# Turning later inputs and router logits on VectorE and DMA instead of TensorE, in a fused attention and feed-forward layer

## The reference

```python
def _L0_attn_ref(x, gamma, w_qkv, w_out):          # 16 heads of 64, DIM 256
    xn = rms_norm(x, gamma)
    qkv = xn @ w_qkv                                # split into q, k, v per head
    sim = jnp.einsum('bhid,bhjd->bhij', q * scale, k)
    out = jnp.einsum('bhij,bhjd->bhid', jax.nn.softmax(sim, axis=-1), v)
    return out.reshape(b, n, DIM_INNER) @ w_out     # after bringing heads back

def _L0_ffn_ref(x, router_w, w1, b1, w2, b2):       # 8 experts, top 2
    router_probs = jax.nn.softmax(xt @ router_w, axis=-1)
    top_k_probs, top_k_indices = jax.lax.top_k(router_probs, TOP_K)
    top_k_probs = top_k_probs / jnp.sum(top_k_probs, axis=-1, keepdims=True)
    expert_out = jax.nn.gelu(xt @ w1 + b1) @ w2 + b2
    return expert_out * jnp.sum(combine, axis=-1, keepdims=True)   # combine: the two weights

x = x + _L0_attn_ref(_layernorm(x), ...)            # x is (8, 512, 256), float32
x = x + _L0_ffn_ref(_layernorm(x), ...)
```

## Time and profile before

| what | us |
|---|---|
| median of 3 runs (1198.33 to 1198.84) | 1198.48 |
| the profiled execution | 1198.14 |
| its span, first to last instruction | 1196.3 |
| TensorE busy / VectorE / ScalarE / GpSimd | 1183.7 / 961.9 / 884.3 / 640.1 |

### The profile page before, as it was taken

The page is one execution under the profiler, slowest core; times in us unless marked ns, Lnnn a source line. Parts: engine busy times, 40 slices in busy tenths (PEclk is TensorE's granted clock), DMA queues, the critical chain, the costliest instruction groups (busy, mean ns, idle before and its releaser), DMA issues. The chain is left out here.

```text
span 1196.3 us, 29198 instructions
## 1 busy us (share of the span) xinstructions
PE 1183.7 (99%) x11347; PEld 1040.4 (87%) x11347; DVE 961.9 (80%) x1714; ACT 884.3 (74%) x1914; POOL 640.1 (54%) x809
## 2 busy tenths in 40 slices
PE   8999999999999999999999999999999999999999
PEld 6778888888888888888888888888888888988988
DVE  7788789878988888888888888889888987666644
ACT  6888788888887888788888887888888884334432
POOL 5776556555655565556555655555555674222221
PEclk9999999999999999999999999999999999999999
DMA  4222111311121113111311131113111232121100
GB/s 132 66 77 66 34 40 30 95 25 35 36 88 35 37 37 89 37 37 37 89 37 36 37 89 37 36 37 89 37 37 37 72 86 79 36 69 39 36 19 36
DMA packets 35240, 62.91 MB, mean 53 GB/s; under 512 B 5920, under 2 KB 12576, under 8 KB 35104
## 3 DMA queue, kind: packets, MB, share of 16 engines
q1 hardware_dynamic: 35104, 61.05, 19.0%
HBM read 19.08 MB, written 8.39 MB: 23 GB/s over the span
## 5 line engine op out<-in xcount | busy, mean ns | idle before, releaser
L927 POOL TENSOR_SCALAR prob<-prob,rowinv 128x512 f32<-128x512 f32 x512 | 350.2, 699 | 290.6 <-DVE rowinv L1116 290.2
L836 ACT ACTIVATE prob<-ps,negmax 128x512 f32<-128x512 f32 x512 | 347.0, 686 | 34.1 <-DVE negmax L1111 29.7
L1035 DVE TENSOR_TENSOR pT_lo<-ps,pT_hi 128x512 fp32r<-128x512 f32 (+1 forms) x384 | 320.4, 862 | 26.0 <-ACT pT_hi L829 21.3
L1111 DVE TENSOR_REDUCE negmax<-ps 128x2 f32<-128x1024 f32 x256 | 311.1, 1215 | 1.3 <-PE ps L524 1.2
L826 ACT ACTIVATE pT_hi<-ps 128x1024 fp32r<-128x1024 f32 x128 | 131.7, 1029 | 99.3 <-issue 98.7
L552 PEld LDWEIGHTS ps<-identity,prob 64*128 64x128 f32 x4096 | 154.7, 138 | 57.9 <-issue 18.2
L552 PE MATMUL ps<-identity,prob 64*128 64x64 f32 x4096 | 177.1, 226 | 3.4 <-DVE vbuf L1035 2.6
L518 PE MATMUL ps<-nat 64*128 64x512 f32 x1024 | 172.1, 413 | 1.5 <-ACT prob L836 0.5
L566 PE MATMUL ps<-pT_hi,vbuf 128*128 128x256 f32 x1024 | 164.8, 283 | 1.7 <-DVE pT_lo L1035 1.6
L566 PE MATMUL ps<-pT_lo,vbuf 128*128 128x256 f32 x1024 | 164.5, 283 | 0.0
L829 ACT ACTIVATE pT_hi<-ps 128x512 fp32r<-128x512 f32 x256 | 140.4, 610 | 16.5 <-PE ps L552 16.5
(11 more groups left out here) (119 smaller groups left out, 2307.1 us busy)
## 6 DMA issues: line engine op xcount, KB each, us to landing
att_hi_v<-halves_out SPq DMA_DIRECT2D x128, 128.0 KB, 2.3
att_lo_v<-halves_out SPq DMA_DIRECT2D x128, 128.0 KB, 2.3
xres<-in_x SPq DMA_DIRECT2D x8, 512.0 KB, 3.4
x_scratch<-xres SPq DMA_DIRECT2D x8, 512.0 KB, 3.1
out_y<-f_o SPq DMA_DIRECT2D x15, 256.0 KB, 2.0
xin<-in_x SPq DMA_DIRECT2D x7, 512.0 KB, 3.8
wstage<-in_w SPq DMA_DIRECT2D x4, 512.0 KB, 3.6
wstage<-in_w_qkv SPq DMA_DIRECT2D x6, 256.0 KB, 3.1
```

What stands on the lines that cost most here:

```text
L836: act.activation(prob[:, n % NPROB, j * SEQ:(j + 1) * SEQ], ps[:, PS_SCORE[n % 2] + j, :], ACT.Exp, bias=negmax[:, n % 4, j:j + 1], accum_ ...
L927: return pool.tensor_scalar(dst, src, scalar, 1.0, ALU.mult, ALU.mult)
L1035: return dve.tensor_tensor(dst, full, hi, ALU.subtract)
L1111: dve.tensor_reduce(negmax[:, n % 4, :], ps[:, PS_SCORE[n % 2]:PS_SCORE[n % 2] + 2, :], AX.X, ALU.max, negate=True).then_inc(s_max, 1)
```

## The change

The input of the first batch is still transposed by TensorE. For the seven later batches and all chunks, VectorE turns the 32x32 blocks of `xn` in place of it (`turn_input`, two instructions), from SBUF to SBUF into `xblocks`; 16 DMAs on SyncE's queue (`spread_input`) then put the blocks where they belong, into the memory of `xn` itself (`xn_turned`). In attention GpSimd makes the hi part from it (`input_hi`) and VectorE the lo part (`input_lo`) at the end of step 13, and the query block of the next batch waits for that. The statistics and normalisation of the next batch start 4 slots earlier. In the feed-forward part `x2_hi` and `ffn_split` read the turned input in SBUF, behind the fourth gelu and the fourth hidden part of the chunk before. The router's product is turned by VectorE from PSUM (`turn_logits`) and spread by 4 DMAs (`spread_logits`), and the product itself stands right behind the last up block, in chunk 0 where it stood. `halves_out` has one buffer of two parts, and the output blocks of even halves stand two steps apart like the odd ones.

Semaphore declarations, changed constants (`NEXT_LN_SLOT = 9`, `SPLIT_STEP = 13`, `QUAD = 32`) and changed indices are left out.

```diff
@@ -81,10 +83,9 @@
...
     for step in range(FIRST_STEP, LAST_STEP + 1):
-        b, rel = divmod(step, SPB_STEPS)
         blocks = []
         if step == -4:
-            blocks += [(2, "xt", 0, 0), (3, "xt", 0, 1)]
+            blocks += [(2, "xt", 0), (3, "xt", 1)]
         if step == -3:
...
@@ -96,13 +97,10 @@
...
             blocks.append((place, "v", step // 4, 1))
-        if rel == 13 and 0 <= b < B:
-            blocks += [(2, "xt", b + 1, 0), (3, "xt", b + 1, 1)]
         for half in range(2 * B - 1):
             since = step - (8 * half + 11)
-            places = {0: 2, 2: 2, 4: 2, 6: 2} if half % 2 else {0: 2, 3: 3, 4: 2, 6: 2}
-            if since in places:
-                blocks.append((places[since], "out", half, list(places).index(since)))
+            if since in (0, 2, 4, 6):
+                blocks.append((2, "out", half, since // 2))
         for place, *task in sorted(blocks):
@@ -159,6 +157,7 @@
...
         xn = sb("xn", [P, TT, D], F32)
+        xblocks = sb("xblocks", [P, KT, TT, P], F32)
...
-        halves_out = sb("halves_out", [P, 2, 2, SEQ], F32, att)
+        halves_out = sb("halves_out", [P, 2, 2, 2 * P], F32, att)
         att_hi_v = sb("att_hi_v", [P, SEQ], F32, att)
@@ -274,6 +275,15 @@
...
+        def block_rows(g, c):
+            return xblocks[g * QUAD:(g + 1) * QUAD, :, :, c * QUAD:(c + 1) * QUAD].rearrange("p k t q -> p (k t) q")
+        def turned_rows(c, g):
+            columns_of_g = xn_turned[c * QUAD:(c + 1) * QUAD].rearrange("p k (t q) -> p (k t) q", t=TT)
+            return columns_of_g[:, :, g * QUAD:(g + 1) * QUAD]
+        N_SPREAD = 16 * (P // QUAD) ** 2
         def aux_bank(block_no):
@@ -366,8 +376,15 @@
         def ln_task(slot):
...
-            b, step = divmod(slot - LN_SLOT, SPB)
-            return (b + 1, step) if step < 9 and 0 <= b + 1 <= B else None
+            if slot < FIRST_SLOT + SPB // 2:
+                return (0, slot - FIRST_SLOT) if 0 <= slot - FIRST_SLOT < 9 else None
+            b, step = divmod(slot - NEXT_LN_SLOT, SPB)
+            return (b + 1, step) if step < 14 and 0 <= b < B else None
+        def split_step(step):
+            b, rel = divmod(step, SPB_STEPS)
+            return b + 1 if rel == SPLIT_STEP and 0 <= b < B else None
...
         def aux_of(step):
...
-                src = halves_out[:, pair % 2]
                 sp.wait_ge(s_halves, 2 * pair + 2)
...
                     sp.wait_ge(s_att, pair)
-                sp.dma_start(att_hi_v[0:DH, :], src[0:DH, 0, :]).then_inc(s_merge, 16)
-                sp.dma_start(att_hi_v[DH:P, :], src[DH:P, 1, :]).then_inc(s_merge, 16)
-                sp.dma_start(att_lo_v[0:DH, :], src[DH:P, 0, :]).then_inc(s_merge, 16)
-                sp.dma_start(att_lo_v[DH:P, :], src[0:DH, 1, :]).then_inc(s_merge, 16)
+                for dst, rows, src_rows, h in ((att_hi_v, 0, 0, 0), (att_hi_v, DH, DH, 1),
+                                               (att_lo_v, 0, DH, 0), (att_lo_v, DH, 0, 1)):
+                    sp.dma_start(dst[rows:rows + DH, :].rearrange("p (a q) -> p a q", a=2),
+                                 halves_out[src_rows:src_rows + DH, :, h, :]).then_inc(s_merge, 16)
+            def spread_input(m):
+                sp.wait_ge(s_blocks, 2 * m)
+                for g in range(P // QUAD):
+                    for c in range(P // QUAD):
+                        sp.dma_start(turned_rows(c, g), block_rows(g, c)).then_inc(s_spread, 16)
...
             def load_x1(c):
...
                 if rel == 24 and b + 2 == B:
-                    sp.wait_ge(s_xn, B - 1)
+                    sp.wait_ge(s_xn, 2 * (B - 1))
                     sp.wait_ge(s_x1, 16)
...
+                if rel == 23 and 0 <= b < B:
+                    spread_input(b + 1)
                 if rel == 19 and 1 <= b < B:
...
+            def spread_logits(c):
+                sp.wait_ge(s_flt, c + 1)
+                if c >= 1:
+                    sp.wait_ge(s_frs, c)
+                blocks = r_blocks[:, :, 0:2 * EXPERTS].rearrange("p (t g) e -> p g t e", t=TT)
+                for g in range(P // QUAD):
+                    sp.dma_start(r_parts[g * QUAD:(g + 1) * QUAD], blocks[:, g]).then_inc(s_frt, 16)
             def store_out(c, part):
...
             sp.dma_start(b2_sb[:, :], b2_rows).then_inc(s_b2, 16)
+            spread_logits(0)
+            spread_input(B + 1)
             sp.wait_ge(s_aux, aux_index[("out", 2 * B - 1, TT - 1)] + 1)
...
             for c in range(B):
+                if c + 1 < B:
+                    spread_logits(c + 1)
+                if c + 2 < B:
+                    spread_input(B + c + 2)
                 store_out(c, 0)
...
-                if kind in "qkv" and block_no >= 4:
-                    pe.wait_ge(s_aux, max(j for (name, *_), j in aux_index.items() if name == "xt" and j < block_no) + 1)
+                if kind == "q" and args[0] % PAIRS == 0 and args[0]:
+                    pe.wait_ge(s_xlo, args[0] // PAIRS)
                 bank = ps[:, aux_bank(block_no), :]
                 if kind == "xt":
-                    b, k = args
...
+                    pe.wait_ge(s_xlo, B)
                 else:
...
-            def transpose_x2(c):
-                pe.wait_ge(s_fx2, c + 1)
-                if c >= 2:
-                    pe.wait_ge(s_fxtlo, c - 1)
-                for k in range(KT):
-                    for t in range(TT):
-                        ins = pe.transpose(ps[:, PS_XT + k, t * P:(t + 1) * P],
-                                           f_x2[:, t, k * P:(k + 1) * P], identity[:, :])
-                ins.then_inc(s_fxt, 1)
             def route(c):
...
                 if c >= 1:
-                    pe.wait_ge(s_frs, c)
+                    pe.wait_ge(s_flt, c)
                 for k in range(KT):
...
-            def transpose_logits(c):
-                pe.wait_ge(s_flt, c + 1)
-                for t in range(TT):
-                    ins = pe.transpose(ps[:, PS_ROUTER, t * 2 * EXPERTS:(t + 1) * 2 * EXPERTS],
-                                       r_logitT[:, t * P:(t + 1) * P], identity[0:2 * EXPERTS, 0:2 * EXPERTS])
-                ins.then_inc(s_frt, 1)
...
             def up(c, f):
...
                     up(c, f)
-                    if c == 0 and f == TAIL_UPS:
-                        transpose_logits(0)
                 if c == 0:
...
                         if block_of_out == last_out[-1]:
-                            pe.wait_ge(s_frs, 1)
+                            pe.wait_ge(s_flt, 1)
                         aux(LAST_STEP + 1, *block_of_out)
                     wait_weight_split(pe, N_CHUNKS - 1)
-                if c + 1 < B:
-                    transpose_x2(c + 1)
-                if c == 0:
                     pe.wait_ge(s_aux, len(aux_index))
+                if 1 <= c < B - 1:
+                    route(c + 1)
                 down(c, 0)
                 down(c, 1)
-                if c + 1 < B:
-                    route(c + 1)
+                if c == 0:
+                    route(1)
                 down(c, 2)
-                if c + 1 < B:
-                    transpose_logits(c + 1)
                 down(c, 3)
...
         def _(act):
...
             def x2_hi(c):
-                act.wait_ge(s_fxt, c)
-                act.activation(f_xT[0][c % 2][:, :, :], ps[:, PS_XT:PS_XT + 2, :], ACT.Copy).then_inc(s_fxthi, 1)
+                act.wait_ge(s_spread, N_SPREAD * (B + c))
+                act.activation(f_xT[0][c % 2][:, :, :], xn_turned, ACT.Copy).then_inc(s_fxthi, 1)
...
             def transposed_hi(n):
...
@@ -841,9 +848,9 @@
             def copy_halves(t):
...
                 act.wait_ge(s_pv, t + 1)
-                if part == 0 and pair >= 2:
-                    act.wait_ge(s_merge, 64 * (pair - 1))
-                act.activation(halves_out[:, pair % 2, :, part * 2 * P:(part + 1) * 2 * P],
+                if part == 0 and pair >= 1:
+                    act.wait_ge(s_merge, 64 * pair)
+                act.activation(halves_out[:, part, :, :],
                                ps[:, PS_OUT, :].rearrange("p (h q) -> p h q", h=2), ACT.Copy).then_inc(s_halves, 1)
...
-            def copy_logits(c):
-                act.wait_ge(s_frm, c + 1)
-                act.activation(r_logitT[:, :], ps[0:2 * EXPERTS, PS_ROUTER, :], ACT.Copy).then_inc(s_flt, 1)
             def router_exp(c):
...
-            copy_logits(0)
             for c in range(B):
...
                     gelu(c * FT + f)
+                    if f == TT - 1 and 1 <= c < B - 1:
+                        x2_hi(c + 1)
                 if c == 0:
                     router_exp(0)
+                    x2_hi(1)
                 if c + 1 < B:
-                    x2_hi(c + 1)
...
+            def input_hi(m):
+                pool.wait_ge(s_spread, N_SPREAD * m)
+                pool.wait_ge(s_auxfull, aux_index[("v", 4 * m - 1, 1)] + 1)
+                for k in range(KT):
```

(82 more changed lines are left out.)

39 lines of the change are left out of this document (15 added, 24 removed).

## The result

The changed kernel takes 1220.89 us (median of 4 runs, 1217.49 to 1222.36), the kernel before 1198.64 beside it: ratio 1.0182, 95% interval 1.0160 to 1.0204. The forecast was 1209, range 1196 to 1217: the sign was right, the size was not (22.2 us lost for the 11.0 of the forecast). The profiled execution of the changed kernel is its fastest, 1217.49, with a span of 1215.7.

The account below looks back on a forecast made before the run. TensorE, busy 99% of the span, was taken to bound the kernel, with SyncE's queue binding the changed feed-forward part. 1198.1 less 2.8 (attention) plus 11.4 (feed-forward) plus 2.4 (long issues) gave 1209.1 us; range 1196 to 1217.

Parts of the forecast that it names:

- The pitch, the landing and the turn: SyncE's 16 transfers follow each other after 0.64 us, the last lands 2.3 later; VectorE's block turn takes 0.70.
- (b): Rival on SyncE's queue: short transfers issue at the early pitch of 0.46; 1196.9 us, chance 0.20.
- (c): Rival: issue costs next to nothing, all 16 under way within 4 us of the turn; 1187 us, chance 0.07.
- (d): Rival: rows of 128 bytes make issue or landing dearer, pitch 0.9; about 1253 us, chance 0.13.
- Long issues: SyncE's feed-forward spreads: two issues 1.2 us longer than the others in seven spreads, 2.4 us lost, bounds 0 and 8.4.
- The feed-forward part: SyncE's queue binds: 11.4 us lost by late chunk inputs, plus 2.4 for long issues.
- 5.3 ahead of the second router product: TensorE stalls 5.3 us before chunk 1's router product, waiting for VectorE's subtraction of the spread input.
- 8.7 in chunk 1's ups: TensorE stalls 8.7 us at chunk 1's seventh up, which starts at 1043.8 instead of 1035.1.
- The attention term: Attention steps 13 and 14: 1.5 us gained per batch, 1.1 lost waiting; 0.4 left, 2.8 for seven.
- the subtractions at 0.70 each: Attention step 13: VectorE's second subtraction takes 0.70 us after GpSimd's multiplications end at 238.2, ending at 238.9.
- The eighth input: Last attention batch: no query and key block behind it, bound by other engines, counted at nothing.
- a remedy: Attention step 13: if VectorE's second subtraction ends a microsecond earlier, attention keeps its 1.5 us per batch.

Follow-up runs that it names:

- half_size: Changed kernel, each of the 16 transfers of a feed-forward spread moving half its bytes, the other half of the turned input left out: 1217.39 us, ratio 1.0159.
- half_issues: Changed kernel, each feed-forward spread issuing 8 of its 16 transfers at whole size, half of the turned input left out: 1199.19 us, ratio 1.0003.
- hi_first_16: Attention part of the change alone, with 16 issues, GpSimd's main parts of the next input put ahead of step 13's tile of scores: 1199.01 us, ratio 1.0006.
- attention_alone: Changed kernel's attention part with the feed-forward part of the kernel before; chunk 0's input turned as in the changed kernel: 1202.55 us, ratio 1.0035.
- the fastest version: Changed kernel, all spreads through DRAM, GpSimd's main parts first, chunk 0's two turns in slots of their own: 1187.62 us, ratio 0.9909.
- by_dram: Changed kernel, its seven feed-forward spreads sent through DRAM by one write and four reads, 5 issues instead of 16: 1199.63 us, ratio 1.0010.
- filled: Changed kernel with 48 matmuls into a bank that nothing reads, put where TensorE stood idle: 1213.80 us.
- ffn_alone: Changed kernel's feed-forward part with the attention part of the kernel before; chunk 0's input comes from TensorE: 1211.28 us, ratio 1.0108.
- all_dram_hi_first: Changed kernel, all spreads through DRAM and GpSimd's main parts of the next input ahead of step 13's tile of scores: 1189.25 us, ratio 0.9923.

## Why the prediction was wrong

*Prices of the new operations.* Right. The pitch, the landing and the turn were read from neighbouring rows and came out at 0.65 to 0.73 for 0.64, 1.9 for 2.3, 0.65 to 0.70 for 0.70. Rivals (b), (c) and (d) are out by these numbers: (b) needed a pitch of 0.46, (c) all 16 under way within 4 us, (d) 0.9. Half the rows and bytes per transfer changed 3.5 us in all (`half_size`). Long issues were forecast as two in seven spreads; the trace has four of 1.2 to 1.6 us.

*The feed-forward part.* Forecast at 13.8 lost with the long issues, measured at 12.6 alone. The mechanism, SyncE's issues as the bound, is shown by `half_issues` and `half_size`. That the size comes so near is in part luck: the measured loss holds the lower clock, which the sum left out. Of its pieces: 5.3 ahead of the second router product were 3.09, since TensorE came there late itself: it stood 2.78 (forecast 0.6) ahead of the first down block, and ran the two down tiles behind it in 7.5 instead of 5.75, partly at the lower clock; 8.7 in chunk 1's ups were 6.4; later chunks wait 0.81 to 1.88 (forecast 1.1). Where nothing waits, the change wins 1.42, not 1.22, of TensorE's time per chunk.

*The attention term failed.* "So 0.4 per batch is left, 2.8 for seven" was 0: the wait is about 1.45 instead of 1.1. GpSimd ends its two multiplications where the forecast has it (238.4 for 238.2, in a trace that runs 0.2 later). The term that was too small is the subtractions at 0.70 each. Side by side the two take 1.84 here and 1.41 in the earlier trace rows, for the same size: the first takes 1.18, while GpSimd makes the other multiplication, and 0.74 to 0.75 before the change. In `hi_first_16`, where both run beside GpSimd's work, both take 1.17. So the second ends 1.2 behind GpSimd and not 0.7, and TensorE's transposes start at 240.07 instead of 239.5. The forecast had reckoned with GpSimd beside VectorE at the normalisation (4.08), but not here.

The eighth input, "I count it at nothing", cost about 3.0, the larger miss: in `attention_alone` steps 120 and 125 to 127 take 8.56, 7.57, 8.46 and 7.95, before 7.46, 7.24, 7.88 and 6.99. The 1.1 of step 120 is the two turns behind the normalisation: the step takes 7.49 in the fastest version, which has them apart. The 1.0 of step 127 is the lower clock: behind a wait of 1.92 the granted clock was 0.79 in that step, and in `by_dram`, with a wait of 1.91 there and the clock at 1.00, the step takes 7.15. With the rest (0.9, spread over single steps) this part stands 6.7 from its forecast.

*A term was missing: TensorE's clock.* The sum took each wait at its length. `filled` shows that work behind the waits then ran at 1.2 GHz, at a cost of 4.8 (traces) to 7.1 us (medians). The clock fell in `ffn_alone` too, and once in `attention_alone`.

*The whole.* The loss is 11.2 us larger than forecast: 6.7 in the attention part and 5.7 by which the two parts cost more together, less the 1.2 by which the feed-forward part alone cost less. Of the 5.7 (2.2 by the spans of the traces) the lateness ahead of the first down block is shown above; how much of the rest is clock, and how much one part's lateness in the other's waits, stays open. The sign came from the feed-forward part; the attention part was forecast to win 2.8 and lost 3.9.

*What the sum said about a remedy* ("If VectorE ends its second subtraction of step 13 a microsecond earlier, attention keeps its 1.5 per batch") held: in `all_dram_hi_first` it ends 1.6 earlier, steps 13 and 14 take 15.06 together instead of 16.5, and the eight inputs give 11.6 us.

The Trainium skill says in "DMA: Bandwidth & Descriptors" (Issuing engines are not separate DMA queues) that initiating a DMA is usually small beside the DMA. For one transfer here it is 0.65 against 1.9; sixteen in a row take 10.4 to 11.7, and the feed-forward part's loss went with their count. Its rule to join small transfers (Rules for kernel authors) is what `by_dram` follows, and the trace agrees.

## What to carry to other kernels

Taking work from the engine that is busy 99% pays only if every engine and queue that replaces it is ready in time. Count the issues of a transfer in a row on their queue, since with 32 KB pieces their number sets the time and not their bytes. Price an operation from a row in which the neighbouring engine is as busy as it will be: VectorE's subtraction took 1.18 beside GpSimd's work and 0.74 without. When a wait is removed, look who was late and not who was waiting: moving the waiting block back made two waits out of one, while moving the late engine's work ahead of a tile that it waited for anyway made 11.6 us. Where a busy TensorE gets a wait of 2 to 4 us, put the slower clock that the work behind it may have into the range: it fell behind most waits of that length here, though not behind all.

## What had not been expected of the hardware

Halving the size of 16 transfers (32 to 16 KB) left their issues at 11.06 us and their landing at 1.8; halving their count took the issues to 5.16. A round trip through DRAM, 2.6 us for a write of 512 KB and 3.2 for the reads, was quicker than spreading within SBUF in 16 pieces. And 48 matmuls that compute nothing made the changed kernel 7 us faster, by keeping the granted clock at 1.00.
